# The tails of a macaron block's two expert layers: rows and gates read where they lie, three of four bank marks issued earlier

## The reference, cut to what matters

```python
x = x + 0.5 * ffn(layernorm(x))      # tail 1 is the end of this one
x = x + attn(layernorm(x))
x = x + 0.5 * ffn(layernorm(x))      # tail 2 is the end of this one

def ffn(x):                          # S = 8192 rows, D = 256, E = 8, FF = 1024
    y1 = ln(x + mha(x))
    gates = softmax(y1 @ wg); idx = argmax(gates)
    keep = place_in_expert < cap     # cap = S // E = 1024 rows for each expert
    z = (y1 @ w1[idx] + b1[idx]) @ w2[idx] + b2[idx]
    return ln(y1 + where(keep, gate * z, 0))
```

## Time and profile before

| | us |
|---|---|
| median of 3 runs | 2764.93 (2763.07 to 2767.3) |
| the profiled execution | 2759.59 |
| its span | 2757.9 |
| PE busy | 2334.6 (85%) |
| DVE busy | 2151.4 (78%) |
| ACT busy | 1657.1 (60%) |
| POOL busy | 838.6 (30%) |

### The profile page before, as it was taken

How to read it: one execution, slowest core, us unless ns; L and a number is a source line. 1 busy time by engine, 2 the same in 40 slices (tenths; PEclk the granted TensorE clock), 3 DMA queues, 4 the chain that set the end, 5 groups by cost and what they waited for, 6 DMA issues and landing times. The chain is left out here.

```text
span 2757.9 us, 45893 instructions
## 1 busy us (share of the span) xinstructions
PE 2334.6 (85%) x15352; PEld 1387.7 (50%) x15352; DVE 2151.4 (78%) x5653; ACT 1657.1 (60%) x3995; POOL 838.6 (30%) x853
## 2 busy tenths in 40 slices
PE   5999998877479969999999999999879999994264
PEld 3666665755345524444444444444656666663243
DVE  5888887827778869889889898888458888887077
ACT  3454544416534429999999999999415445452154
POOL 2353433264734430000000000000123343431746
PEclk8999999878889969999999999999989999997677
DMA  4132214283235565445455455452441121211722
GB/s 122 52 97 77 70 47 145 102 271 115 84 126 172 168 126 103 94 102 108 95 106 106 94 105 104 96 107 60 130 153 54 47 69 47 69 47 52 210 73 77
DMA packets 244683, 281.54 MB, mean 102 GB/s; under 512 B 41808, under 2 KB 212880, under 8 KB 243808
## 3 DMA queue, kind: packets, MB, share of 16 engines
q1 hardware_dynamic: 217712, 218.02, 31.1%
q0 software_dynamic: 16384, 50.35, 5.7%
q10 hardware_dynamic: 10352, 10.23, 1.3%
HBM read 190.63 MB, written 94.16 MB: 103 GB/s over the span
## 5 line engine op out<-in xcount | busy, mean ns | idle before, releaser
L2202 DVE CUSTOM_DVE_ANT_0 banks<-banks,attn_bias 128x128 f32<-128x128 f32 (+7 forms) x1024 | 759.7, 778 | 108.1 <-PE banks L1909 82.8
L2115 ACT ACTIVATE attn_probT<-banks 128x512 f32<-128x512 f32 x1152 | 622.5, 621 | 61.2 <-PE banks L1926 50.9
L1909 PE MATMUL banks<-attn_kst,attn_qst 96*128 96x512 bf16 (+3 forms) x1536 | 421.4, 336 | 22.3 <-DMA attn_qst<-qparts 12.3
L1926 PE MATMUL banks<-attn_qst,attn_kst 99*128 99x256 bf16 (+3 forms) x2176 | 410.9, 281 | 15.3 <-ACT attn_probT L2115 7.1
L1948 PE MATMUL banks<-attn_probT,attn_vb 128*32 128x256 f32 (+3 forms) x4352 | 315.6, 400 | 7.9 <-ACT attn_probT L2115 7.3
L1926 PEld LDWEIGHTS banks<-attn_qst,attn_kst 99*128 99x128 bf16 x2176 | 187.3, 97 | 169.3 <-ACT attn_probT L2115 54.9
L2260 POOL CAST attn_lowp<-attn_lowT 128x32 bf16<-128x32 f32 x64 | 13.4, 209 | 850.3 <-DVE attn_lowT L2210 850.3
L410 PE MATMUL banks<-ffn_xT,winT 128*128 128x512 f32 x512 | 250.7, 612 | 6.5 <-ACT ffn_w L610 2.9
L1909 PEld LDWEIGHTS banks<-attn_kst,attn_qst 96*128 96x128 bf16 x1536 | 117.4, 97 | 255.6 <-DVE attn_low L2202 158.1
L2103 ACT COPY banks<-attn_biasT 128x512 f32<-128x512 f32 x384 | 227.8, 628 | 27.9 <-DMA attn_biasT<-neardT 21.2
L870 POOL TENSOR_TENSOR ffn_xs<-ffn_xs,row_ffn_out 128x1024 f32<-128x1024 f32 x32 | 75.4, 2356 | 412.3 <-DVE ffn_xs L752 386.5
(11 more groups left out here) (254 smaller groups left out, 4507.9 us busy)
## 6 DMA issues: line engine op xcount, KB each, us to landing
rows<-ffn_xs SPq DMA_DIRECT2D x64, 512.0 KB, 3.1
attn_qst<-qparts SPq DMA_DIRECT2D x384, 64.0 KB, 2.8
attn_kst<-kparts SPq DMA_DIRECT2D x186, 128.0 KB, 5.0
ffn_xs<-in_L_ffn_w_dram SPq DMA_DIRECT2D x16, 1024.0 KB
attn_biasT<-neardT SPq DMA_DIRECT2D x128, 128.0 KB, 5.0
attn_bias<-neard SPq DMA_DIRECT2D x128, 128.0 KB, 2.2
qparts<-qkv_part SPq DMA_DIRECT2D x32, 384.0 KB, 2.8
kparts<-qkv_part SPq DMA_DIRECT2D x32, 384.0 KB, 2.8
```

Of the source, the lines that this page charges most:

```text
L1909: mm = nc.tensor.matmul(score[k % 2][:, a:e], qst[0:K6, u, half, hh, ii * P:(ii + 1) * P], kst[0:K6, u, hh, a:e], start=True, stop=True)
L1926: mm = nc.tensor.matmul(tbank[t % 3][:, at:at + nb * P], kst[:, u, hh, j * P:(j + 1) * P], qst[:, u, half, hh, x:x + nb * P], start=(k == ...
L2115: nc.scalar.activation(probT[:, g % 2, i, 0:w], tbank[t % 3][:, 0:w], ACT.Exp, scale=-1.0).then_inc(s_exp, 1)
L2202: nc.vector.tensor_tensor_reduce(out=part, in0=part, in1=bias[:, hh, T - w:T], scale=1.0, scalar=BIG, op0=ALU.add, op1=ALU.min, accum_out= ...
```

## The change

Three edits. `place` is gone: `transposes` reads the rows of xs itself, and waits for the gather's semaphore (`got`) in place of the copy's. The tile gnow is gone: `sums` takes its scalar straight from the column of the tile gates. And in tail 1 the four marks are taken apart: those of banks 7 and 4 go ahead of the last but one bias_sum, that of bank 5 ahead of the last one, and only that of bank 6 stays behind the last bias_out; ACT's `seeds(0, 0)` there waits for three marks, `seeds(1, 1)` for four. In tail 2 the four marks stand together as before. The tile y1 is now called w1T0 and only holds turned weights and what it lends.

```diff
@@ tiles @@
-        y1 = ph.sb("y1", [P, 2, GT, C])
+        w1T0 = ph.sb("w1T0", [P, FB, C])
-        gnow = ph.sb("gnow", [P, 2, GT])
@@ ACT @@
-            def place(n, u):
-
-                got(act, n, u)
-                if not under(n, 2):
-                    act.wait_ge(s_tps, 2 * n - 2)
-                act.nop(nofuse=True)
-                nc.scalar.copy(y1[:, u, :, :], all_rows(n, 0, C)).then_inc(s_y1, 1)
...
             def start_seeds():
                 act.wait_ge(s_w, 32 if turn else 16)
+                if turn == 0:
+                    act.wait_ge(s_b12sb, 1)
+                act.wait_ge(s_marked, 4 if turn else 3)
+                seeds(0, 0)
                 act.wait_ge(s_marked, 4)
-                seeds(0, 0)
                 seeds(1, 1)
...
             def body(n, u):
-                if not ends(n, 2):
-                    place(n + 2, u)
@@ PE @@
             def transposes(n, u):
-                pe.wait_ge(s_y1, n + 1)
+                got(pe, n, u)
...
-                                                 y1[:, u, t, k * P:(k + 1) * P], core.ident[:, :])
+                                                 row(n, t, k * P, (k + 1) * P), core.ident[:, :])
...
+            def mark(*banks):
+
+                for b in banks:
+                    nc.tensor.matmul(bank[b], core.ones[:, :], w12[:, 0, 0:2 * C], start=True, stop=True).then_inc(s_marked, 1)
...
                 transposes(0, 0)
+                pe.wait_ge(s_inv, 1)
+                pe.wait_ge(s_w12sb, NE - 1)
+                mark(7, 4)
                 bias_sum(NE - 2)
+                pe.wait_ge(s_w12sb, NE)
+                mark(5)
                 bias_sum(NE - 1)
-                pe.wait_ge(s_w12sb, NE)
                 pe.wait_ge(s_b12sb, NE)
+                mark(6)
@@ DVE @@
             def sums(n, u):
                 got(dve, n, u)
                 wait_apart(dve, s_zps, 2 * n + 1)
-                nc.vector.tensor_copy(gnow[:, u, :], gates[:, bass.ds(n * GT, GT)]).then_inc(s_gnow, 1)
-                wait_apart(dve, s_gnow, n + 1)
...
-                            scalar=gnow[:, u, t:t + 1], in1=row(n, t, 0, C), op0=ALU.mult, op1=ALU.add)
+                            scalar=gates[:, n * GT + t:n * GT + t + 1], in1=row(n, t, 0, C), op0=ALU.mult, op1=ALU.add)
```

More of the change, by code:

```diff
@@ L983, in ffn @@
         s_w = ph.sem("w")
-        y1 = ph.sb("y1", [P, 2, GT, C])
+        w1T0 = ph.sb("w1T0", [P, FB, C])
         xT = ph.sb("xT", [P, 2, KB, GW])
-        w1T = [y1[:, :, :, :].rearrange("p u t c -> p (u t) c"),
+        w1T = [w1T0[:, :, :],
                xT[:, :, :, :].rearrange("p u k (h c) -> p (u k h) c", c=C)]
@@ L999, in ffn @@
                                 "marked", "seed"))
-        gnow = ph.sb("gnow", [P, 2, GT])
-        s_gnow, s_mine, s_y1 = ph.sem("gnow"), ph.sem("mine"), ph.sem("y1")
+        s_mine = ph.sem("mine")
         bank = [core.ps[:, i, :] for i in range(8)]
@@ L1045, in ffn @@
                 Lent(xT[:, :, :, :].rearrange("p u k c -> p (u k c)")),
-                Lent(y1[:, :, :, :].rearrange("p u t c -> p (u t c)")), Lent(flat[:, 7 * ROWS:8 * ROWS]))
+                Lent(w1T0[:, :, :].rearrange("p f c -> p (f c)")), Lent(flat[:, 7 * ROWS:8 * ROWS]))
         attend_sync, attend_tensor, attend_scalar, attend_vector, attend_gpsimd, over_yet, stored = ffn_attention(
@@ L1184, in _ @@
                 for e in range(2, NE):
-                    if e == NE - 1:
-                        place(0, 0)
-                        place(1, 1)
                     w12_out(e)
@@ L1304, in _ @@
                 pe.wait_ge(s_w, 32)
[L1305 to L1308, removed]
+                pe.wait_ge(s_inv, 1)
+                mark(4, 5, 6, 7)
             def products(n, u):
```

## The result

The changed kernel takes 2757.34 us (median of 20 runs) and the kernel before 2765.53 (20 runs beside it). The ratio is 0.9969, 95% interval 0.9963 to 0.9975: 8.6 us faster (6.9 to 10.2). The forecast was 10.8 us faster, a median of 2754.1 us.

A forecast was written before the change was run, and what follows sets the result against it. The prediction took DVE to set the pace in both tails, though PE is busiest on the page. Gates 6.0, rows 2.0 and marks 2.8 sum to 10.8 us, taking the median from 2764.93 to 2754.1 us; range 2746 to 2763.

The forecast's parts named there:

- The gates: DVE's steps in both tails: without the gates' copy a step falls from 6.51 to 6.31 us; 6.0 us saved.
- The rows: Start of each tail: without ACT's copies 1.0 us saved in each, 2.0 us in all; nothing in steady steps.
- The marks: Way into tail 1: one mark, not four, behind the last bias, so products start at 633.4, not 636.26; 2.8 us.
- the 3.5 forecast: Sign in tail 1: first products some 3.5 us behind the start of the one mark, where they came 6.3 behind the four.
- POOL didn't become the bound: Rival, both tails: fourth store held through two DVE instructions, POOL's step 7.3 us, kernel slower at 2780.6 us; chance 0.10.
- with 2.6 needed: POOL's fourth store in a step: from 2.6 us on it decides against the change.
- The number of groups done under the gathers: Rivals, tail 2: one group more done while gathers run, 2747.8 us, chance 0.13; one less, 2760.4 us, chance 0.11.
- The copies weren't hidden: Rival: the copies were hidden, first sums start as late as before, only the marks count, 2762.1 us; chance 0.13.
- The rule weighed: POOL's fourth store: taken strictly, held through both two-input DVE instructions, L1486 and L1489; the trace agreed for the first alone.

The follow-up runs named there:

- the kernel with pauses: Changed kernel plus three small GpSimd fills before each group's four gathers and before the first 13 (tail 1) and 7 (tail 2) store groups: 2722.20 us, ratio 0.9850.
- the other three with copies: Kernel before with rows still copied by ACT: gates read in place, ratio 0.9991; three marks moved ahead, 0.9993; both edits, 0.9972.
- three parts alone: Kernel before with one edit each: gates read in place, ratio 0.9991; rows transposed where they lie, 1.0004; three marks moved ahead, 0.9993.
- two together: Kernel before with gates read in place and three marks moved ahead, rows still copied by ACT: ratio 0.9972.
- the changed kernel again: The changed kernel, unaltered, measured a second time against the kernel before: ratio 0.9974, 7.2 us faster.
- both in turns: Changed kernel with tail 2's gathers and stores alternating on GpSimd after six groups gathered ahead: ratio 0.9978.
- paced by the products: Changed kernel with tail 2's gathers, from the fifth group on, waiting for the products of the group four before: ratio 0.9931.

## Why the prediction was right, and where its sizes were off

- **The gates, 6.0 us forecast.** The mechanism held: the copy goes, the sums follow at 1.14 us, the step shrinks. The size was off. The step fell by 0.13 us and not 0.20, since the EPS addition behind the sums now starts 0.64 us into a store of POOL where it had started 0.84 us into it; it takes 0.13 us longer and the reciprocal 0.05, which overlap to 0.07. In the eleven steps from group 4 on the whole change gave 71.87 - 70.20 = 1.7 us in tail 1 and 72.12 - 70.18 = 1.9 in tail 2, 3.6 in all; 0.75 of that are three longer steps of before, which belong to the rows, so the gates gave 22 x 0.13 = 2.9 us there. The forecast had checked whether DVE's earlier instructions would hold POOL, not whether POOL would hold them. That the 0.20 was there to be had, the kernel with pauses shows with its 6.31 us.
- **The rows, 2.0 us forecast.** 0.8 us at the head of tail 1 in every profile, at that of tail 2 between nothing and 0.8, and nothing that the times resolve. The forecast held that in the steady steps ACT's copies are worth nothing. There it was wrong: they left PE without slack for its slower products, at a price of 0.75 us in the profile of before and 1.1 to 1.9 in the other three with copies.
- **The marks, 2.8 us forecast.** 3.2 us on average. PE's first products 2.84 us behind the start of the last mark were within the 3.5 forecast. The forecast had transposes at the lower clock and products at the higher; the products' clock varies from run to run.
- **The sum.** In the two profiles 3.6 + 1.6, and 3.2 for the marks, make 8.4 us by the stretches; 8.6 by the times, 10.8 forecast. The difference is mostly the gates' term. That 8.4 and 8.6 lie so close is partly luck, since the marks' worth and the head of tail 2 each vary by more than that.
- **The rivals.** POOL didn't become the bound: the fourth store took 1.86 us, with 2.6 needed. The number of groups done under the gathers stayed at one. The copies weren't hidden: the step fell.
- **The rule weighed.** The fourth store starts at 688.64 and ends at 690.50, inside the second of DVE's two instructions (689.70 to 690.93), so that one doesn't hold it; the rows of before had shown the same. GPSIMD Engine Reference, Specifications, of the Trainium skill states contention with DVE instructions that have two SBUF inputs; the trace agrees for the first of the two alone.
- **The level.** The 5.3 us between the profiled execution of before and its median were carried over as they were. That much spread is usual: the spans of the next five profiles (three parts alone, two together, the changed kernel again) lie between 2753.7 and 2766.5 us, with 5.6 us of that in the stretch from the end of the attention to the index of tail 2, which none of the changes touches.

## What to carry to other kernels

When an instruction goes from the pace-setting engine, everything behind it starts earlier against the other engines' rhythm; read which of its short instructions then fall into what they had just missed. Work taken from an engine that isn't the bottleneck can still pay in the rare steps in which another engine is slow. An idle engine's filler can have a second use: four marks cost 5.5 us, but the products behind them found a full clock (taking three of them away from there still gained 3.2 us). And when all engines stop at once without a releaser, look at what one queue does without a pause, before trimming the work around it: three small fills in POOL's queue were worth more than three times the whole change.

## What the runs showed of the hardware

- **Indirect DMAs issued by GpSimd without a pause stop the other engines.** PE, DVE and ACT stood with one issue every 1.25 us (gathers of 256 KB), 1.28 us (stores of 128 KB, 100 GB/s), 1.31 and 1.34 us (both in turns) and 1.30 us (a pause of 0.49 us every four). In tail 1 of the changed kernel PE began to slow down at 576.4 us, behind 22 us of one issue every 1.33 to 1.37 us (a pause of 1 us every eight). They ran freely with one every 1.48 to 1.6 us (a pause of 1.2 us every four; of 3.0 us every eight; paced by the products), at up to 376 GB/s beside it. It sets in some 14 to 25 us after an unpaused row of issues begins, and ends 3 to 7 us after POOL's stopping: in tail 1 of the changed kernel POOL stops at 600.90 us and PE runs again from 605.31. That something fills up when issues come faster than about one in 1.4 us, between 1.37 and 1.48, fits all of this, but no run shows what it is; whether it is the pause or the mean rate that counts wasn't separated either.
- **A short DVE instruction is held until GpSimd's issue is almost over.** The EPS addition on 128 x 4 takes 0.17 us. Over all fourteen profiles, when it starts 0.53 to 0.78 us into an indirect DMA's issue (0.94 to 0.98 us long), it ends 0.93 to 0.96 us behind the start of that issue: it takes 0.41 us from 0.53, 0.31 from 0.63, 0.20 from 0.73 and 0.17 from 0.78 on. From 0.79 us to the issue's end no issue holds it, and of the 21 that started within the first 0.50 us 19 took less than 0.2 us. A fill can hold it too: in the last three groups of the kernel with pauses before the stores it takes 0.30 to 0.36 us, starting around the start of one.
